# Attention sums with the ones in the value weights: three heads in one matmul round, the fourth in a second

## What is computed

```python
q_proj = _elu1(jnp.einsum('bhnd,hdf->bhnf', q, proj_matrix))
k_proj = _elu1(jnp.einsum('bhnd,hdf->bhnf', k, proj_matrix))
kv = jnp.einsum('bhnf,bhnd->bhfd', k_proj, v)
attn = jnp.einsum('bhnf,bhfd->bhnd', q_proj, kv)
k_sum = k_proj.sum(axis=2)
z = 1.0 / (jnp.einsum('bhnf,bhf->bhn', q_proj, k_sum) + 1e-08)
attn = attn * z[..., None]
```

## Time and profile before

| | |
|---|---|
| device time, median of 3 runs | 312.54 us (312.38 to 314.48) |
| the profiled execution's own device time | 312.71 us |
| its span, first to last instruction | 311.0 us |
| TensorE matmul busy | 285.5 us, 92% of the span |
| VectorE, ScalarE, GpSimd busy | 211.7, 191.2, 176.6 us |
| chain of work that ended last | TensorE 64%, VectorE 20%, issue 7% |
| L540, the sums, of that chain | 5% |

### The profile page before, as it was taken

How to read it: one execution, slowest core, us unless ns; L and a number is a source line. 1 busy time by engine, 2 the same in 40 slices (tenths; PEclk the granted TensorE clock), 3 DMA queues, 4 the chain that set the end, 5 groups by cost and what they waited for, 6 DMA issues and landing times.

```text
span 311.0 us, 8859 instructions
## 1 busy us (share of the span) xinstructions
PE 285.5 (92%) x2556; PEld 254.3 (82%) x2556; DVE 211.7 (68%) x821; ACT 191.2 (61%) x511; POOL 176.6 (57%) x201
## 2 busy tenths in 40 slices
PE   8899999999999999997999999999999999999600
PEld 7788787868778786876989899999999999999500
DVE  1655868686887898688575766554444688888761
ACT  4686567567656766656446555555566565878742
POOL 2400217656566756666536777777777547666730
PEclk9999999999999999999999999999999999999955
DMA  5990002021021002332101133333322644563151
GB/s 137 349 293 14 34 4 60 28 64 34 33 65 37 26 29 75 78 88 62 37 17 36 47 97 100 97 102 97 107 85 70 206 129 141 163 182 116 49 169 35
DMA packets 23553, 27.92 MB, mean 90 GB/s; under 512 B 4248, under 2 KB 16580, under 8 KB 23506
## 3 DMA queue, kind: packets, MB, share of 16 engines
q1 hardware_dynamic: 19186, 18.82, 21.3%
q0 software_dynamic: 4320, 8.53, 8.2%
HBM read 16.17 MB, written 11.62 MB: 89 GB/s over the span
## 4 chain that ended last, share of the span: by engine, by line
PE 64%; DVE 20%; issue 7%; DVEq 4%; POOL 2%; ACT 1%; POOLq 0%; ACTq 0%
PE pair L638 13%; PE bank L658 6%; PE pair L658 6%; PE bank L562 6%; PE bank L540 5%; PE pair L493 4%; DVEq L1095 3%; PE pair L495 3%; PE pair L494 3%; PE bank L605 3%; PE bank L586 3%; PE bank L506 3%; PE bank L582 3%; DVE k_feat L939 2%; DVE z L1250 2%
## 5 line engine op out<-in xcount | busy, mean ns | idle before, releaser
L882 ACT ACTIVATE h<-pair,w_t 128x128 f32<-128x128 f32 x284 | 81.2, 369 | 53.4 <-PE pair L638 53.4
L382 POOL DMA_INDIRECT routed_rows<-x,slot_of x64 | 68.1, 1065 | 43.9 <-issue 37.0
L405 POOL DMA_INDIRECT expert_rows<-y_sb,xt x71 | 71.3, 1004 | 32.3 <-DVE y_sb L1233 17.8
L638 PE MATMUL pair<-xtT,w_t 128*128 128x128 f32 x568 | 75.9, 277 | 2.7 <-DVE w_t L1101 1.7
L638 PEld LDWEIGHTS pair<-xtT,w_t 128*128 128x128 f32 x568 | 69.0, 192 | 4.2 <-DVE w_t L1101 3.9
L1101 DVE COPY w_t<-w_sb 128x516 f32 x71 | 31.3, 441 | 25.5 <-issue 24.3
L800 ACT ACTIVATE expo<-pair 128x1024 f32<-128x1024 f32 x32 | 32.9, 1027 | 25.5 <-PE pair L495 25.5
L658 PE MATMUL pair<-w_sb,h 128*128 x288 | 38.3, 276 | 0.4 <-ACT h L882 0.4
L658 PE MATMUL bank<-w_sb,h 128*128 x280 | 37.4, 276 | 0.0
L658 PEld LDWEIGHTS pair<-w_sb,h 128*128 128x128 f32 x288 | 35.0, 192 | 0.6 <-issue 0.6
L658 PEld LDWEIGHTS bank<-w_sb,h 128*128 128x128 f32 x280 | 34.0, 192 | 0.2
(11 more groups left out here) (187 smaller groups left out, 473.0 us busy)
## 6 DMA issues: line engine op xcount, KB each, us to landing
xt<-routed_rows SPq DMA_DIRECT2D x71, 66.0 KB, 2.0
yb<-expert_rows SPq DMA_DIRECT2D x7, 512.0 KB, 3.5
x_tok<-in_L_attn_x_dram SPq DMA_DIRECT2D x8, 256.0 KB, 2.7
w_sb<-in_L_ffn_W_dram SPq DMA_DIRECT2D x1, 2048.0 KB, 10.1
out_dram<-z SPq DMA_DIRECT2D x7, 256.0 KB, 2.8
expert_rows<-y_sb,xt POOLq DMA_INDIRECT x71, 2.3
routed_rows<-x,slot_of POOLq DMA_INDIRECT x64, 2.3
routed_rows<-pad_rows SPq DMA_DIRECT2D x8, 66.0 KB
```

What stands on the lines that cost most here:

```text
L382: pool.indirect_dma_start(out=xs_dram, out_offset=bass.IndirectOffsetOnAxis(ap=slot_of[:, s, t, k:k + 1], axis=0), in_=x2[:, s * T + t, :] ...
L405: pool.indirect_dma_start(out=y_dram, out_offset=bass.IndirectOffsetOnAxis(ap=xt_u[:, i % XR, D:D + 1], axis=0), in_=y_sb[:, i % YR, :], i ...
L638: mm = nc.tensor.matmul(B[i % 2][:, cols(c)], w1_t[:, i % WR, cols(c)], xtT[:, i % 2, :], start=True, stop=True)
L882: ins = nc.scalar.activation(h[:, i % 2, cols(c)], B[i % 2][:, cols(c)], ACT.Gelu, bias=w1_t[:, i % WR, F + c:F + c + 1])
```

## The change

The ones go into the weights. A head's 8 values and one column of ones are 9 columns; three heads make 27 and fit into a group of 32, the fourth doesn't. So `v_sb` and `ones_f` give way to `v_three` (three heads of 9 columns in each chunk's 32, the rest zero) and `v_last` (the fourth head's 9 columns, the rest zero). Round 0 of the sums streams the 96 features of the three heads past `v_three`, round 1 the 32 features of the fourth past `v_last`. The result is 128 wide, is turned in one transpose, and is copied to `kv_bd` in two pieces by partitions (96 and 32). The zeros of `kv_bd` outside these blocks, of the weights and the ones are written once at the start by GpSimd, and `take_values(0)` waits for them (`s_zero`). The mask is made from a new table `ahead`. In the loop and at the start both last queries now come ahead of both rounds.

```diff
+            nc.gpsimd.memset(v_three[:, :, :, :], 0.0).then_inc(s_zero, 1)
+            nc.gpsimd.memset(v_last[:, :, :, :], 0.0).then_inc(s_zero, 1)
+            nc.gpsimd.memset(kv_bd[:, :, :, :], 0.0).then_inc(s_zero, 1)
+            nc.gpsimd.memset(ahead[:, :, :], 1.0).then_inc(s_ahead, 1)
+            pool.wait_ge(s_zero, 3)
+            nc.gpsimd.memset(v_three_h[:, :, :, HD:VW], 1.0).then_inc(s_zero, 1)
+            nc.gpsimd.memset(v_last_g[:, :, HD:VW], 1.0).then_inc(s_zero, 1)
...
-                at = slice(i * P, i * P + P)
+                v = v_three if i == 0 else v_last
+                at = slice(0, (HC - 1) * FEAT) if i == 0 else slice((HC - 1) * FEAT, P)
                 for t in range(T):
                     for c in range(FC):
-                        rows = slice(c * HC * HD, (c + 1) * HC * HD)
-                        w = v_sb[:, t, rows] if i == 0 else ones_f[:, :]
-                        mm = nc.tensor.matmul(B[5][rows, at], w, k_feat[:, t, cols(c)], start=(t == 0),
-                                              stop=(t == T - 1), tile_position=(0, c * HC * HD))
+                        rows = slice(c * GV, (c + 1) * GV)
+                        mm = nc.tensor.matmul(B[5][rows, at], v[:, t, c, :], k_feat[:, t, cols(c)][:, at],
+                                              start=(t == 0), stop=(t == T - 1), tile_position=(0, c * GV))
...
-                for i in range(2):
-                    mm = nc.tensor.transpose(B[3][:, cols(i)], kv_t[:, i, :, :].rearrange("p h f -> p (h f)"),
-                                             ident[:, :])
-                mm.then_inc(s_kv_ps, 1)
+                nc.tensor.transpose(B[3][:, 0:P], kv_t[:, :, :].rearrange("p h f -> p (h f)"), ident[:, :])\
+                    .then_inc(s_kv_ps, 1)
...
                 queries(s, 1, 0)
+                queries(s, 1, 1)
                 sum_keys_values(s, 0)
-                queries(s, 1, 1)
                 if s == SEQS - 1:
                     transpose_tile(0)
                 sum_keys_values(s, 1)
...
+                m = (HC - 1) * FEAT
+                sums = B[3][:, 0:P].rearrange("p (c m) -> p c m", c=FC)
+                nc.scalar.activation(kv_bd[0:m, :, 0:HC - 1, :].rearrange("p c j i -> p c (j i)"),
+                                     sums[0:m, :, 0:(HC - 1) * VW], ACT.Copy)
+                nc.scalar.activation(kv_bd[m:P, :, HC - 1, :], sums[m:P, :, 0:VW], ACT.Copy).then_inc(s_kv_bd, 1)
...
                 dve.wait_ge(s_v, s + 1)
                 wait_if(dve, s_kv, s)
-                nc.vector.tensor_copy(v_sb[:, :, :].rearrange("p t d -> p (t d)"), B[4]).then_inc(s_v_sb, 1)
+                if s == 0:
+                    dve.wait_ge(s_zero, 5)
+                v = B[4].rearrange("p (g h i) -> p g h i", h=HC, i=HD)
+                nc.vector.tensor_copy(v_three_h[:, :, :, 0:HD], v[:, :, 0:HC - 1, :])
+                nc.vector.tensor_copy(v_last_g[:, :, 0:HD], v[:, :, HC - 1, :]).then_inc(s_v_sb, 1)
```

More of the change, by code:

```diff
@@ L92, in build_layer @@
         kv_mask = sb("kv_mask", [P, HC])
-        ones_f = sb("ones_f", [P, HC * HD])
+        ahead = sb("ahead", [P, FC, HC - 1])
         minus_half = sb("minus_half", [P, T])
@@ L124, in build_layer @@
         xT_hi, xT_lo = sb("xT_hi", [P, 2, N], F32R), sb("xT_lo", [P, 2, N], F32R)
-        v_sb = sb("v_sb", [P, T, D])
+        GV = HC * HD
+        v_three, v_last = sb("v_three", [P, T, FC, GV]), sb("v_last", [P, T, FC, GV])
+        v_three_h = v_three[:, :, :, 0:(HC - 1) * VW].rearrange("p t c (h i) -> p (t c) h i", i=VW)
+        v_last_g = v_last[:, :, :, :].rearrange("p t c m -> p (t c) m")
         expo = sb("expo", [P, 2, 2 * NF])
@@ L129, in build_layer @@
         q_feat = sb("q_feat", [P, FC, N])
-        kv_t = sb("kv_t", [P, 2, HC, FEAT])
+        kv_t = sb("kv_t", [P, HC, FEAT])
         kv_bd = sb("kv_bd", [P, FC, HC, VW])
@@ L203, in build_layer @@
         s_warm = sem("s_warm")
+        s_zero, s_ahead = sem("s_zero"), sem("s_ahead")
         s_proj_bd = sem("s_proj_bd")
@@ L443, in _ @@
             nc.gpsimd.tensor_scalar(e_cap[:, :], iota8[:, 0, 0, :], float(CAP), None, ALU.mult).then_inc(s_dest, 1)
+            nc.gpsimd.memset(v_three[:, :, :, :], 0.0).then_inc(s_zero, 1)
[5 more added lines that the diff above has]
+            nc.gpsimd.memset(v_last_g[:, :, HD:VW], 1.0).then_inc(s_zero, 1)
+            pool.wait_ge(s_ahead, 1)
+            nc.gpsimd.affine_select(out=ahead[:, :, :], in_=ahead[:, :, :], compare_op=ALU.is_ge, fill=0.0, base=0,
+                                    pattern=[[-GV, FC], [-VW, HC - 1]], channel_multiplier=1).then_inc(s_ahead, 1)
+            pool.wait_ge(s_ahead, 2)
+            nc.gpsimd.affine_select(out=ahead[:, :, :], in_=ahead[:, :, :], compare_op=ALU.is_ge, fill=0.0,
+                                    base=VW - 1, pattern=[[GV, FC], [VW, HC - 1]], channel_multiplier=-1)\
+                .then_inc(s_ahead, 1)
             pool.wait_ge(s_dest, 14)
@@ L667, in _ @@
             keep_warm(6, B[0])
-            pe.wait_ge(s_const, 10)
+            pe.wait_ge(s_const, 9)
             pe.wait_ge(s_in_qkv, 32)
@@ L805, in take_sums @@
                 wait_if(act, s_num, 2 * s)
-                sums = B[3][:, 0:2 * P].rearrange("p (k c j i) -> p k c j i", k=2, c=FC, j=HC)
-                nc.scalar.activation(kv_bd[:, :, :, 0:HD], sums[:, 0, :, :, :], ACT.Copy)
-                nc.scalar.activation(kv_bd[:, :, :, HD], sums[:, 1, :, :, 0], ACT.Copy).then_inc(s_kv_bd, 1)
+                if s == 0:
+                    act.wait_ge(s_zero, 3)
+                m = (HC - 1) * FEAT
[3 more added lines that the diff above has]
+                nc.scalar.activation(kv_bd[m:P, :, HC - 1, :], sums[m:P, :, 0:VW], ACT.Copy).then_inc(s_kv_bd, 1)
             def attention_T(s):
@@ L946, in mask_key_values @@
                 wait_if(dve, s_kv_ps, s)
[L947 to L950, removed]
+                nc.vector.tensor_tensor(kv_t[:, :, :], B[5][:, 0:P].rearrange("p (j f) -> p j f", j=HC),
+                                        kv_mask[:, :].unsqueeze(2).broadcast_to([P, HC, FEAT]), ALU.mult)\
+                    .then_inc(s_kv_t, 1)
             def normalize_heads(s, i):
@@ L1162, in _ @@
             nc.vector.memset(squares[:, 0, :], 0.0).then_inc(s_warm, 1)
-            dve.wait_ge(s_const, 10)
+            dve.wait_ge(s_const, 9)
             dve.wait_ge(s_in_qkv, 32)
@@ L1186, in _ @@
                 .then_inc(s_sim, 1)
+            dve.wait_ge(s_ahead, 3)
+            nc.vector.memset(kv_mask[:, HC - 1:HC], 1.0).then_inc(s_kv_mask, 1)
+            nc.vector.tensor_reduce(kv_mask[:, 0:HC - 1], ahead[:, :, :].rearrange("p c j -> p j c"), AX.X, ALU.add)\
+                .then_inc(s_kv_mask, 1)
             features(0, 0)
@@ L1190, in _ @@
             x_low(1)
-            dve.wait_ge(s_kv_mask, 1)
+            dve.wait_ge(s_kv_mask, 2)
             mask_key_values(0)
```

10 lines of the change are left out of this document (4 added, 6 removed).

## The result

| | before | after |
|---|---|---|
| device time, median of 20 executions each | 312.81 us (311.78 to 315.24) | 315.24 us (313.30 to 320.79) |
| profiled execution's own time, its span | 312.71, 311.0 us | 313.38, 311.6 us |
| mean granted clock of the profiled execution | 0.976 | 0.973 |

The ratio of the comparisons is 1.0052, 95% interval 1.0030 to 1.0073: some 1.6 us more, within 1% as forecast. (Three executions of after took over 320 us at a lower mean clock; the ratio leaves them out, the median has them.) On the 312.54 us from which the forecast was made the ratio gives 314.2 us, near the upper end of the range of 311.0 to 314.5; the median itself is 2.5 us over the forecast time and 0.7 us above the range.

The account below looks back on a forecast made before the run. It took the wait before the x2 transposes, set by GpSimd's power and norm_rows, to bound a turn. Start +2.22 us, loop and tail -2.12 us: +0.10 us, forecast 312.7 us, range 311.0 to 314.5.

Parts of the forecast that it names:

- What bounds a turn: Loop: the 0.48 us between x2 ready and TensorE reaching L592, not TensorE's saving, says how much of a turn can go.
- at TensorE's least saving the result would be the same: Loop: TensorE saving only 0.33 us a turn, instead of 1.34, would still give the 0.34 us gain.
- the 1.01 us taken in proportion to the columns: Rounds of the sums on TensorE: from 1.01 us each to 0.76 and 0.25 us, saving 1.01 us a turn.
- 0.34 us a turn: Loop: gain at the end of the x2 transposes, 91.05 for 91.39; 1.85 us over six turns.
- it ends 90.34: VectorE's norm_rows in a turn: starts at 89.23 for 89.36, 0.13 us sooner, and so ends at 90.34.
- The power: GpSimd's power ahead of norm_rows: no sooner, held up by x_low, which isn't moved; its end 0.30 us behind x_low's.
- A freed power: Loop: with a power of 1.20 us norm_rows would wait for the mask instead and a turn gain 0.52 us.
- The start's wait: Start: take_values(0) waits for GpSimd's five fills; +2.22 us on the first query and all that follows.
- The start's clock: Start: rival that the granted clock falls in TensorE's 2.2 us without matmuls, +3.4 us, 316.1 us; chance 0.05.
- after the last matmul the clock stood at 1.00 through 3.1 us with none: Kernel's end: trace evidence taken to show that the start's gap is too short for the clock to fall.
- till it is back: Start, clock rival: about 1 us more lost until the clock recovers, part of its 3.4 us.
- The tail: Seventh turn to the first up (L638): last relu comes sooner, late w_t is next; 0.27 us gained.

Follow-up runs that it names:

- e5: Kernel before with only the loop's order changed: second of the last queries ahead of round 0; median 311.51 us, ratio 0.995.
- e4: e1 (packed sums, fills early) with the last query again between the two rounds, against the kernel before; median 311.17 us, ratio 0.989.
- e9: e1 with VectorE's first q_feat of a turn moved behind norm_rows in all turns but the last; 310.99 us, ratio 0.990 to the kernel before.
- e2: Changed kernel with ten idle matmuls of zeros on TensorE in the gap ahead of L705; 315.83 us, ratio 1.005 to the kernel before.
- e1: Changed kernel with GpSimd's six fills and two selects moved ahead of its wait for s_sim; 310.61 us, ratio 0.991 to the kernel before.
- e8: The changed kernel run once more, unaltered, beside the kernel before; 315.03 us, ratio 1.004.
- e11: e9, but q_feat keeps its old place in the turn followed by the first list of tiles; 307.56 us, ratio 0.981 to the kernel before.
- e6: e1 with GpSimd's scatter of the last quarter of first choices held until x2 is done; 331.42 us, ratio 1.047 to the kernel before.
- e7: e1 with VectorE's mask of the sums ahead of x_low in seven turns; 310.05 us, ratio 0.987 to the kernel before.
- e3: Kernel before with only the start's wait added: five same-size fills that the first copy of the values awaits; 318.06 us, ratio 1.015.

## Why the prediction came out as it did

- **What bounds a turn: right.** Neither half of the change, nor both, moves the turn by more than the wait before `transpose_x2` lets it; "at TensorE's least saving the result would be the same" is what e5 and e4 show. The measured saving of the rounds, 0.93 us, is close to the 1.01 us taken in proportion to the columns.
- **0.34 us a turn: half of it.** The start of `norm_rows` came as forecast (M + 4.33, 0.14 sooner for 0.13). The term that failed is "it ends 90.34", which kept its length at 1.11 us: started 0.13 us sooner against GpSimd's scatter, which lay over it before too, its fourth operation took 515 for 340 ns. That left 0.17 us in four turns, and 0.20 in the turn with the first list, where 0.15 was forecast; turn 1, where no scatter runs, gained the full 0.34 and 0.13 more that only the packed kernels have (0.47 in all).
- **The power: right for this change, for a wrong reason.** It did not come sooner, but not because `x_low` stayed. It is held by the instruction with two SBUF inputs that runs as it starts, here `q_feat`, and ends 0.90 us behind that one's end. (A freed power was to give a turn 0.52 us; in e9 the turns gained 0.7, but there `q_feat` moved away too.) The Trainium skill (SBUF — State Buffer, Who interferes with whom) names such pairs, and the trace agrees; which of two was the holder, I decided from one coincidence of ends, seen twice.
- **The start's wait: right.** 2.44 us for 2.22. The fills follow each other at 0.47 and 0.46 us where I had 0.45.
- **The start's clock: wrong, and the largest miss.** The rival was there, with 0.05. What failed is the step "after the last matmul the clock stood at 1.00 through 3.1 us with none": from one gap behind steady work I concluded that 2.2 us are safe. In after the matmuls ahead of the gap are themselves sparse (0.96 us of idle before 8.17), and the clock fell 0.5 us after TensorE had resumed; that the sparse matmuls make the difference is argued, no run varies them. The Trainium skill (TensorE: Matmul & The Clock Gate, Why this matters for your kernels) warns of idle gaps between bursts of matmuls; here three profiles with gaps of 2.13 to 2.29 us have the fall. Its price, 1.35 us against before and 1.47 against e2, is less than the 3.4 I gave that rival: from L705 to the exponential it took 3.96 us for 2.44, not twice as long, and for the 1 us "till it is back" no row stood.
- **The tail: right at the place named,** -0.29 us for -0.27, and `w_t` is what is late next. That M(7) comes another 0.4 us sooner I had left out; e5 and e4 show that it is the packing's.
- **Open:** profiled +0.6 us, by all comparisons +1.2 to +1.6. Of after's 20 executions only two had the mean clock of the profiled one, 0.973; most had 0.962 to 0.968. A stretch of 3.41 us at 0.50 takes about 0.0055 off the mean over 311 us (an estimate from these two numbers), so most had one or two more than the profiled one. One place for them shows in the profiles: before the first `up`, L655, TensorE idles 1.59 us in the packed kernels, where it idled 1.00 us before, and in e1, e8 and e11 a stretch begins 0.1 to 0.9 us behind it and M(6) to M(7) takes 20.93 to 20.98 us for 19.97. In after, e2, e4, e6, e7 and e9 the same gap stands and the clock stays at 1.00 behind it: the gap alone doesn't decide, and what does, the runs don't show. The 0.5 us behind M(7) are unexplained too.

## What to carry over

When an engine is freed, look not only at what it waits for next but at what that next work will lie beside once it moves: half of this gain was lost because the rows began 0.13 us sooner against a scatter that had not stretched them before. Put one-time fills where their engine waits anyway, and a wait of 2 us in TensorE's way at the start is to be priced with the clock. A saving that falls into a wait is not lost: find what holds the awaited work (here one `q_feat`), and the same packing that gave nothing in a turn gives 0.35 us.

## What the runs showed of the hardware

- GpSimd's power of 4 elements takes 1.01 to 1.07 us in the loop when no such instruction runs as it starts, and 1.16 to 2.12 us if VectorE then runs one with two SBUF inputs (`q_feat`, `k_feat`, `x_low`): it ends 0.90 to 0.91 us behind that one's end, in turns 1 to 6 of all thirteen profiles (in turn 7 0.98 to 1.06 us). A `k_feat` that started 0.08 to 0.98 us later did nothing to it (1.04 to 1.07 us). The copy `w_t`, with one SBUF input, is not harmless: when it lay over the power's end in turn 7 (before, e1), the power ended 0.04 us behind it. In e7 a start 0.03 us behind `k_feat` gave 2.08 us for `inv_norm`, in e1 a start 0.59 us ahead of it gave 1.05; this is the long turn of e7 (18.76 us), first e7, then e1:

```profile
129.91 1.21 DVE L964 SCALAR_TENSOR_TENSOR k_feat<-expo,relu 128x1024 f32<-128x1024 f32 x1
129.94 2.08 POOL L372 TENSOR_TENSOR inv_norm<-norm_c,minus_half 128x4 f32<-128x4 f32 x1
```

```profile
129.69 1.05 POOL L372 TENSOR_TENSOR inv_norm<-norm_c,minus_half 128x4 f32<-128x4 f32 x1
130.28 1.22 DVE L964 SCALAR_TENSOR_TENSOR k_feat<-expo,relu 128x1024 f32<-128x1024 f32 x1
```

- GpSimd's indirect scatter (1.0 to 1.1 us of issue) can stretch a VectorE `tensor_scalar` of 128 elements, SBUF to SBUF, from 340 to 515 ns. Of the four rows beside it at most one took over 400 ns in the loop's turns 1 to 6: in after the fourth, which starts 0.61 us behind the scatter's start, and in before none, where the rows start some 0.03 us ahead of it and 0.22, 0.48 and 0.74 us behind it.
- From 12 us to the last matmuls, the five gaps of TensorE over 2 us (2.13, 2.21, 2.29, and 2.77 and 3.00 in e6) all had a fall of the granted clock, within them or up to 1.7 us behind them. Of the twelve gaps of 1.46 to 1.62 us four had one within 1 us, so such a gap can do without. A fall needs no long gap either: in e9 it came behind 0.60 us, in e3 (156.57) 5.5 us behind the last gap over 0.1 us. In e9 it stayed at 0.50 for 13.65 us although TensorE had no pause in the 11.7 us of the row above.
